# Routing a chunk inside attention: a mixed attention and expert kernel on one Trainium2 core

## The reference

```
x = x + 0.5 * expert(layernorm(x))      # experts, first time
x = x + attention0(layernorm(x))        # causal, 16 heads of 8, own wq, wk, wv, wo, bo
x = x + 0.5 * expert(layernorm(x))      # experts, second time
x = x + 0.5 * ternary(layernorm(x))
x = x + attention1(layernorm(x))        # causal, 16 heads, joint qkv with bias, no output projection
x = x + 0.5 * ternary(layernorm(x))

expert(h):  e = argmax(h @ Wr.T)        # 8 experts, one for each token
            y = gelu(h @ W1[e] + b1[e]) @ Wo + bo + h
            return layernorm(y) * gamma + beta
ternary(h): relu(h @ quantize(W1).T + b1) @ quantize(W2).T + b2
```

## Time and profile before

| | us |
|---|---|
| median of 3 runs | 1184.02 (1182.99 to 1186.48) |
| profiled execution, its time | 1181.55 |
| its span from first to last instruction | 1179.7 |
| TensorE matmuls busy | 1058.8 (90%) |
| VectorE busy | 973.2 (82%) |
| ScalarE busy | 662.1 (56%) |
| GpSimd busy | 100.6 (9%) |
| load of a sorted tile (64 KB), issue to landing | 1.8 |
| store of sorted rows (256 KB) | 2.3 |
| load of query rows (512 KB) | 3.7 |

### The profile page before, as it was taken

One profiled execution on the slowest core, in us unless ns is written; L12 is line 12 of the kernel. 1 busy time (PEld: TensorE's weight loads), 2 busy tenths in 40 slices (PEclk: granted clock), 3 DMA queues, 4 the chain that ended last, 5 costly groups with the idle time before them and its releaser, 6 DMA issues.

```text
span 1179.7 us, 34486 instructions
## 1 busy us (share of the span) xinstructions
PE 1058.8 (90%) x14718; PEld 484.9 (41%) x14718; DVE 973.2 (82%) x2307; ACT 662.1 (56%) x852; POOL 100.6 (9%) x124
## 2 busy tenths in 40 slices
PE   4989968999999999999788848699999999999988
PEld 2545533333333333334447726233333333333436
DVE  7786579999999999986535766899999999998843
ACT  3322214556777777787414213256677777787763
POOL 1530010000000000000043152000000000000000
PEclk9999989999999999999898979899999999999999
DMA  5061142000000000000011032210000000000001
GB/s 163 2 274 47 48 141 65 3 3 2 3 2 2 3 3 3 2 3 3 1 39 38 25 90 81 86 43 3 3 2 3 3 2 2 3 2 3 3 3 37
DMA packets 29493, 36.68 MB, mean 31 GB/s; under 512 B 3694, under 2 KB 26388, under 8 KB 29084
## 3 DMA queue, kind: packets, MB, share of 16 engines
q1 hardware_dynamic: 27228, 29.22, 7.4%
q0 software_dynamic: 2112, 5.25, 1.7%
HBM read 15.29 MB, written 18.87 MB: 29 GB/s over the span
## 4 chain that ended last, share of the span: by engine, by line
PE 50%; DVE 38%; issue 4%; ACT 3%; DMA 1%; SPq 1%; another core or an unknown queue 1%; POOL 0%; DVEq 0%; ACTq 0%; POOLq 0%
DVE part_max L2071 28%; PE psum L1930 12%; PE psum L1951 11%; PE psum L1901 6%; PE psum L520 5%; PE psum L1916 2%; PE psum L1583 2%; ACT hidden L2033 2%; PE psum L1978 1%; DVE xn L204 1%; PE psum L1182 1%; PE psum L544 1%; PE psum L1957 1%; PE psum L1573 1%; PE psum L299 1%
## 5 line engine op out<-in xcount | busy, mean ns | idle before, releaser
L2071 DVE TENSOR_REDUCE part_max<-psum 128x1 f32<-128x512 f32 (+3 forms) x1120 | 675.6, 669 | 37.5 <-PE psum L1957 21.8
L2033 ACT ACTIVATE hidden<-psum 128x1024 f32<-128x1024 f32 (+3 forms) x640 | 539.1, 895 | 221.4 <-PE psum L1901 220.6
L1951 PE MATMUL psum<-k_slots,q_slots 128*32 128x512 f16 (+3 forms) x5120 | 389.1, 353 | 27.8 <-DVE part_max L2071 15.1
L1930 PE MATMUL psum<-hidden,v_aug 128*9 128x512 f32 (+3 forms) x2560 | 291.3, 532 | 0.1
L1951 PEld LDWEIGHTS psum<-k_slots,q_slots 128*32 128x32 f16 x5120 | 123.0, 95 | 285.2 <-DVE part_max L2071 202.2
L1901 PE MATMUL psum<-q_slots,k_slots 32*128 32x512 f16 (+3 forms) x1472 | 140.5, 328 | 9.5 <-ACT hidden L2033 7.9
L520 PE MATMUL psum<-parts,w_parts 128*128 128x512 f16 x384 | 91.2, 389 | 3.8 <-DVE parts L945 3.8
L1957 PE MATMUL psum<-ident_bf,later_keys 128*32 128x128 bf16 (+2 forms) x1408 | 90.2, 247 | 0.0
L1901 PEld LDWEIGHTS psum<-q_slots,k_slots 32*128 32x128 f16 x1472 | 42.0, 91 | 98.7 <-ACT hidden L2033 46.3
L1916 PE MATMUL psum<-later_keys,ident_bf 128*32 128x128 bf16 x2048 | 75.1, 223 | 4.4 <-ACT hidden L2033 1.9
L1930 PEld LDWEIGHTS psum<-hidden,v_aug 128*9 128x9 f32 x2560 | 61.8, 91 | 34.5 <-ACT hidden L2033 1.9
(11 more groups left out here) (278 smaller groups left out, 846.8 us busy)
## 6 DMA issues: line engine op xcount, KB each, us to landing
expert_regions<-k_slots SPq DMA_DIRECT2D x2, 4096.0 KB, 17.8
q_slots<-q_rows SPq DMA_DIRECT2D x8, 512.0 KB, 3.7
k_slots<-k_rows POOLq DMA_DIRECT2D x28, 128.0 KB, 4.1
q_slots<-in_L_ffn_W_dram SPq DMA_DIRECT2D x2, 1024.0 KB, 6.4
q_rows<-parts SPq DMA_DIRECT2D x6, 256.0 KB, 2.6
k_rows<-parts SPq DMA_DIRECT2D x6, 256.0 KB, 2.7
q_slots<-expert_regions SPq DMA_DIRECT2D x20, 64.0 KB, 1.8
sorted_rows<-xn SPq DMA_DIRECT2D x5, 256.0 KB, 2.3
```

The source lines that it names most:

```text
L1930: last = pe.matmul(psum[VW * h:VW * h + DH + 1, O_BANK, off:CH], v_aug[:, j, G * g + h, :], probs[:, (2 * n + h // 2) % NP, h % 2, off:CH] ...
L1951: last = pe.matmul(psum[rows32(m), bank, a * w:(a + 1) * w], q_slots[:, g, qb * P + m * SLOT:qb * P + (m + 1) * SLOT], k_slots[:, G * g + ...
L2033: act.activation(probs[:, tile % NP, :, off:CH], psum[:, bank:bank + 2, off:CH], ACT.Exp, scale=scale).then_inc(exp_done, 1)
L2071: dve.tensor_reduce(part_max[:, step_no[s] % 2, h0:h0 + heads, i, kc], psum[:, bank, 0:heads * w].rearrange("p (a k) -> p a k", a=heads), ...
```

## The change

1. *Dense chunk inside attention 0.* A new class `DenseChunk` holds the dense chunk's buffers, semaphores and steps. Two ring items are added: "dense turn" in turn 158 (turn on PE, two copies on ScalarE behind that turn's exponentials, low part on DVE) and "dense logits" in turn 160 (four matmul blocks on PE, copy and choice on DVE). In turn 167 PE makes mask 0 before the last projection; DVE adds the bias before it waits for the projection, for all projections, and at the last one it also masks the input for expert 0 there.
2. *Sorting layer reordered.* PE starts with mask 1 and expert 0, without waiting for `released`; the wait, the choices' turn and the turns of the early chunks stand in the middle of expert 0, their logits behind it, ranks, late turn, late logits, ranks and tables in and behind experts 1 to 4. One mask bank (4) serves all masks instead of two.
3. *One turn later.* `features.turn(pe, 0)` comes behind the down projection of the last group of tiles.
4. *Ternary layer 1.* DVE's low part 1 comes before the whole norm of the next chunk, not between its statistics and its end.
5. *Last ternary layer.* Ring items "feature" 0 and 1 in turns 158 and 160 of attention 1: turn on PE, high part on ScalarE, low part on DVE. The up projection of chunk 0 is issued in turn 164, behind the last values, before the last output is turned. The layer then starts with up 1 and waits for `released` only before its third turn.

```diff
+            def mask_of(self, pe, e):
+                pe.wait_ge(self.chosen, 1)
+                if e >= 1:
+                    pe.wait_ge(self.mask_ready, e)
...
-                pe.wait_ge(*released)
                 early = batches[0]
-                turn(dense, PREP_BANK)
-                turn(early[0], BATCH_BANK)
-                turn(early[1], SPARE_BANK)
-                logits([dense], PREP_BANK)
-                logits(early, BATCH_BANK)
-                pe.wait_ge(chosen, 1)
-                for e in range(AHEAD_E):
-                    mask_of(e)
-                choices()
...
+                def beside(e):
                     if e == 0:
+                        dense_chunk.mask_of(pe, 2)
+                        pe.wait_ge(*released)
+                        choices()
+                        turn(early[0], BATCH_BANK)
+                        turn(early[1], SPARE_BANK)
+                    if e == 1:
+                        ranks(0, BATCH_BANK)
+                    if e == 2:
+                        logits([late], PREP_BANK)
+                    if e == 3:
+                        ranks(1, PREP_BANK)
+                    if e == 4:
+                        table(2)
+
+                def following(e):
+                    if e == 0:
+                        logits(early, BATCH_BANK)
+                    if e == 1:
                         pe.wait_ge(choices_out, 1)
                         turn(late, PREP_BANK)
+                    if e + 3 < E:
+                        dense_chunk.mask_of(pe, e + 3)
+                    if e == 3:
+                        table(1)
+                    if e == 4:
+                        table(3)
+
+                dense_chunk.mask_of(pe, 1)
+                for e in range(E):
+                    masked_expert(e, lambda: beside(e))
+                    following(e)
                 table(4)
                 biases()
...
+                    down(n)
                     if n == TGROUPS - 1:
                         features.turn(pe, 0)
-                    down(n)
...
                     following.low_parts(dve, 0)
-                    norms.begin(dve, own, s1, order[2])
                     features.low_part(dve, 1)
-                    norms.end(dve, own, s1, order[2])
+                    norms.make(dve, own, s1, order[2])
...
+            if dense:
+                ahead_items = [("dense turn", 0), ("dense logits", 0)]
+            else:
+                ahead_items = [("feature", 0), ("feature", 1)]
...
+                RING_ITEMS[-1] += {LAST_QUAD - 5: ahead_items[:1], LAST_QUAD - 3: ahead_items[1:]}.get(len(RING_ITEMS) - 1, [])
...
+                        if dense and item == final:
+                            dense.mask_of(pe, 0)
                         ring_item(item)
...
+                    if features and turn == LAST_QUAD + 1:
+                        pe.wait_ge(ring_read, ring_no["feature", 0] + 1)
+                        features.up(pe, 0)
...
+                        if kind == "project":
+                            rows = x_res[:, what * BPC:(what + 1) * BPC, :]
+                            own(dve.tensor_tensor(rows, rows, bcast_blocks(bo_bc, BPC), ALU.add))
+                            if item == final:
+                                dense.masked(dve, 0)
                         dve.wait_ge(ring_full, n + 1)
```

More of the change, by code:

```diff
@@ L1148, in sorted_turn @@
                     else:
[L1149 removed]
+                        pe.wait_ge(mask_ready, E)
                     for i in range(BPC):
@@ new lines, in low_part_of, with up @@
+            def low_part_of(self, dve, n, bank):
+                dve.wait_ge(self.hi_ready, n + 1)
+                return dve.scalar_tensor_tensor(out=self.x_parts[:, n % 2, 1, :], in0=psum[:, bank, :], scalar=X_SCALE,
+                                                in1=self.x_parts[:, n % 2, 0, :], op0=ALU.mult, op1=ALU.subtract)
+            def low_part(self, dve, n):
+                self.low_part_of(dve, n, 4 + n % 2).then_inc(self.lo_ready, 1)
+            def up(self, pe, n, relu_done=None):
+                if n >= self.begun:
+                    pe.wait_ge(self.lo_ready, n + 1 - self.begun)
+                for t in range(HT):
+                    if n >= 1:
+                        pe.wait_ge(relu_done, HT * (n - 1) + t + 1)
+                    for xp in range(2):
+                        last = pe.matmul(psum[:, t, :], tw1_t[:, t, :], self.x_parts[:, n % 2, xp, :],
+                                         start=(xp == 0), stop=(xp == 1))
+                    last.then_inc(self.up_done, 1)
@@ L1567, in up @@
                 def up(n):
[L1568 to L1575 removed]
+                    features.up(pe, n, relu_done)
                 def down(n):
@@ L1605, in _ @@
                 else:
-                    pe.wait_ge(*released)
-                    features.turn(pe, 0)
-                    for n in range(NCH):
+                    pe.wait_ge(*features.last_split)
+                    for n in range(1, NCH):
                         up(n)
+                        if n == 1:
+                            pe.wait_ge(*released)
                         if n + 1 < NCH:
                             features.turn(pe, n + 1)
-                        if n >= 1:
-                            down(n - 1)
+                        down(n - 1)
                     down(NCH - 1)
@@ L1687, in _ @@
                 else:
-                    late = list(norms.order[given:])
-                    for n in range(NCH - 1):
-                        features.low_part(dve, n)
-                        if late:
-                            norms.make(dve, own, s1, late.pop(0))
+                    norms.begin(dve, own, s1, order[NCH - 1])
+                    features.low_part(dve, 2)
+                    norms.end(dve, own, s1, order[NCH - 1])
                     dve.wait_ge(norms.ready, NB)
@@ L1963, in ring_item @@
                         last = pe.transpose(psum[0:G * BPC, bank, 0:P], neg_max[:, k % 2, :], ident[:, :])
+                    elif kind == "dense turn":
+                        last = dense.turn(pe, bank)
+                    elif kind == "dense logits":
+                        last = dense.logits(pe, bank)
+                    elif kind == "feature":
+                        last = features.turn_into(pe, what, bank)
                     elif kind == "turned":
@@ L2041, in _ @@
                         act.copy(out_t[:, k % 2, :], psum[:, O_BANK, :]).then_inc(out_copied, 1)
+                    for kind, what in items:
+                        n = ring_no[kind, what]
+                        if kind == "dense turn":
+                            act.wait_ge(ring_full, n + 1)
+                            dense.copies(act, RING_BANKS + n % RING)
+                        elif kind == "feature":
+                            act.wait_ge(ring_full, n + 1)
+                            features.high_part_of(act, what, RING_BANKS + n % RING)
             @blk.vector
@@ L2066, in _ @@
                         bank = RING_BANKS + n % RING
-                        dve.wait_ge(ring_full, n + 1)
-                        if kind == "scores":
+                        if kind == "project":
[3 more added lines that the diff above has]
+                                dense.masked(dve, 0)
+                        dve.wait_ge(ring_full, n + 1)
+                        if kind == "dense turn":
+                            dense.low_part(dve).then_inc(ring_read, 1)
+                            dve.wait_ge(ring_read, n + 1)
+                        elif kind == "dense logits":
+                            dve.tensor_copy(dense.logit[:, 0:BPC, :],
+                                            psum[:, bank, 0:BPC * E].rearrange("p (b e) -> p b e", e=E)).then_inc(ring_read, 1)
+                            dve.wait_ge(ring_read, n + 1)
+                            dense.choose(dve, own, dense.place, BPC, NPART)
+                        elif kind == "feature":
+                            features.low_part_of(dve, what, bank).then_inc(ring_read, 1)
+                        elif kind == "scores":
                             s, i, kc, h0, heads = what
@@ L2076, in _ @@
                         elif kind == "project":
-                            rows = x_res[:, what * BPC:(what + 1) * BPC, :]
-                            own(dve.tensor_tensor(rows, rows, bcast_blocks(bo_bc, BPC), ALU.add))
                             own.wait()
```

255 lines of the change are left out of this document (131 added, 124 removed).

## The result

| | before | after |
|---|---|---|
| median of 4 runs, us | 1183.66 (1182.99 to 1186.48) | 1161.27 (1159.16 to 1164.12) |
| profiled execution, its time | 1181.55 | 1162.20 |
| its span | 1179.7 | 1160.4 |
| TensorE / VectorE busy | 1058.8 / 973.2 | 1054.0 / 972.7 |
| mean granted clock | 0.971 | 0.975 |

The medians differ by 22.4 us. The profiled executions differ by 19.3, against 19.0 forecast. TensorE and VectorE are busy for nearly as long as before; what went is mostly waiting.

What follows compares the result with a forecast made beforehand. The prediction took waits at five places, behind attention 0 through to the end, as what the change could shorten. Gains 0 + 9.0 + 4.1 + 0 + 5.9 = 19.0 us gave 1162.6 profiled, 1165.0 for the median, range 1159 to 1173.

Steps and rivals of the forecast that it cites:

- what attention 0 pays: Dense chunk's added work inside attention 0: 0.7 lost against clock won back, taken as 0, ends 1.2 lost and 0.7 won.
- part 1: Dense chunk moved inside attention 0, sorting layer reordered: sorted-row loads start earlier, 9.0 us gained, ends 5.3 and 10.
- part 2: Turn placed behind the last sorted group's down projection, which then needn't wait: 4.1 us gained, ends 3.0 and 4.3.
- part 3: Low part before the norm in ternary layer 1: 0 gained, ends 1.5 lost and 2.5 won.
- part 4: Last ternary layer's first two splits moved into attention 1: 6.8 less 0.9 paid there, 5.9 us gained, ends 5.3 and 7.
- Boundary: Behind attention 0: first masked expert starts at 578.5 instead of 588.56, 10 us earlier; first scatter from 588.5 instead of 594.55.
- the scatters become what is late: Sorting: table complete at 601.3 without late signals, scatters land 605.6, so loads start at 605.7 instead of 615.20: 9.5 us.
- rival A: Signals to DVE and ScalarE late twice or more on the table's chain: 9.0 becomes 5.4, time 1168.6; chance 0.27.
- The further 0.3: Sorting: TensorE's pause at 617 to 621 shrinks and with it time at the lower clock, 0.3 us gained.
- Rival B: Maskings and choices beside scatters lock GpSimd out of the shared port, lengthening scatters by 1.5 to 2 us: 1167; chance 0.10.
- Rival D: Some ten TensorE signals beside scatters each late by 3.0: 30 lost against 19 won, 1195, slower; chance 0.03.
- the 0.9 that attention 1 was to pay: Two turns and two high parts added in attention 1, 1.2 in all, less 0 to 1.4 for clock: 0.9 lost.

Runs made afterwards that it cites:

- the second chip: Chip of four follow-up kernels: scatters held back, tiny probe operations, idle matmuls in the changed kernel or with the last-layer edit undone; the kernel before took 1177.58 there.
- without part 3: Changed kernel with DVE's low part 1 in ternary layer 1 again between the statistics and the end of the norm: 1163.35, ratio 0.986.
- the held version: Changed kernel with GpSimd waiting for the finished table before the first scatter: 1168.24, and 1170.67 when run again on a third chip.
- without parts 2, 3 and 4: Three kernels, each the changed kernel with one edit undone (later turn, ternary layer 1's low part, last ternary layer): 1168.29, 1163.35, 1173.76.
- the kernel without part 4: Changed kernel without the two feature items in attention 1 and the up projection ahead: 1173.76, ratio 0.993.

## Why the prediction was right, and where it was not

Predicted 1165.0 (1159 to 1173), measured 1161.27. By the profiled executions the sum was 1162.6 and the time is 1162.2. The sum is right because its errors cancel:

| term | forecast | before to after | with the part taken away |
|---|---|---|---|
| what attention 0 pays | 0 | 0.4 gained | 0.6 gained |
| part 1 at the boundary and in sorting | 9.0 | 6.6 | 7.2 |
| part 2 | 4.1 | 3.9 | 4.2 |
| part 3 | 0 | 1.0 | 1.1 |
| part 4 with attention 1 | 5.9 | 7.3 | 9.1 |

(Part 1 from the last maximum to the first down projection of sorted rows, 72.4 before and 65.8 after; part 2 from there to the `x_plus` addition behind group 4, 44.1 and 40.1; part 3 from there to attention 1's first maximum, 74.2 and 73.2; part 4 from there to the end, 433.1 and 425.8.) They sum to 19.3 with 0.04 from the start. That the sum comes so close is luck in part: part 1 was forecast 2.4 too high, parts 3 and 4 together 2.4 too low.

**Attention 0** pays nothing, as taken. The drop of the clock in 560 to 570 is gone: the window stands at 1.00 in after, and a drop comes behind it instead.

**Boundary.** Expert 0 came 10.3 earlier, forecast 10. The first scatter came 6.8 earlier, forecast 6; the twelfth at 602.19, forecast 603.1; SyncE's reads took 2.42, forecast 2.4. These steps held.

**The term that was mis-sized** is part 1's 9.0, and in it "the scatters become what is late", with one late signal of 3.0 to 3.2 assumed on the table's chain. There was one, but 5.9 long, so the table was late (605.5) and not the scatters; rival A's mechanism with one event in place of two, though it priced two at 5.4 where 6.6 came. The price of one signal was also too low by the prediction's own figures: 3.0 to 3.2 against a slack of 2.0 (603.7 to 605.7) cost 1.0 to 1.2, not 0.8. Without a late signal the step holds: on the second chip the loads start 50.7 and 50.1 behind the last maximum, where the forecast's 605.7 is 49.7. With it they stand at 52.4 and 54.0. The further 0.3 for the clock in 617 to 621 didn't come: the clock averages 0.76 in the 14 us from 606 in after, as in the 14 us from 613 before.

**How long the late signals last.** All traces with late signals at the table have one thing in common. In the kernel before (timeline, 608 to 613), the last scatter is issued from 609.19 to 610.16, and TensorE had finished the table's third step at 608.95:

```profile
612.12 0.17 DVE L1405 TENSOR_TENSOR tile_f<-psum,tile_rank 1x20 f32<-1x20 f32 x1 [2.79 <-remote]
```

VectorE takes it up 2.0 us after the issue of the last scatter ended. In after this is 1.7 us, without part 3 it is 2.1, and in all nine traces with late signals there it is 1.7 to 2.1, though TensorE had finished at very different times, from 4.2 us before the end of that issue to 0.3 behind it. So a fixed length of 3.0 to 3.2 was the wrong model: the table came when the scatters were over, and the loads start 5.6 to 6.1 behind the start of the last scatter in all nine (5.9 before, 5.7 in after), against 2.3 to 3.1 in the traces of the second chip. What part 1 brought to the loads, 7.3 us, is by this reading the 7.0 by which the scatters moved. It is read from the traces; no run was made to test it.

**Rival B, the port rule.** The Trainium skill (SBUF — State Buffer, section "SBUF: two separate sides") gives the shared port, for the whole instruction, to whichever of the two engines starts first. The prediction charged every masking in full, also those that begin while a scatter runs, which the page doesn't ask for. Three maskings fell beside scatters, not four, which the prediction's reading of the rule would price at 2.1. The twelve scatters take 1.004 us on average in after and 0.988 in the held version, with one masking beside them: 0.2 in all. Only a masking that began just ahead of a scatter cost something (592.77 and 592.97: 1.33 instead of 0.96). Those begun while a scatter ran (589.25 and 596.18) cost nothing, as the page has it for GpSimd. But they weren't blocked by the scatter either: the one at 589.25 started as soon as its mask was copied and took its usual 0.69. The row was the better guide.

**Rival D** asked for late signals beside scatters from ten of TensorE's signals. The mechanism exists, but with at most five of them in a trace, several released together, and none beside the first five scatters. In the traces without parts 2, 3 and 4 it also held TensorE up, by 1.7 and 2.8 us, without moving the loads by more than 0.5.

**Part 2** is right in each step: the down projection without a wait, the turn covered, 4.2 forecast for the down's end.

**Part 3** failed in one step: "since the turn's place is set by the norm, which doesn't move". The norm's statistics had waited 1.55 in the earlier trace rows, and the low part fills that wait. The turn came 1.7 earlier against the `x_plus` addition (36.8 behind it before, 35.1 after), and the lower clock on the down projection took 0.7 back (5.36 against 4.61 without part 3). The result lies inside the ends given.

**Part 4.** 23.0 forecast from the last values to the end, 22.6 measured. What was wrong is the 0.9 that attention 1 was to pay: it was 0.45 by the kernel without part 4, and the fall of the clock in the earlier trace rows stayed away, which gave 1.3 that don't belong to the part. The larger worth with the part taken away is the clock again, 2.8 of it.

**The median.** The forecast put it 2.5 above the profiled execution, as before. It is 0.9 below it. The same kernel's medians differ by 0.7 between two chips, before's by 6, so this last addition had no ground.

## What to carry to other kernels

Read which wait ends last after the change as carefully as the one you remove. Here the gain at the loads was 7 and not the 9.5 of the forecast without late signals, because a late signal, which the trace of before already showed twice, stayed on the path. Its length changed, but its end hardly moved against the end of the last scatter (2.0 before, 1.7 after). So compare the end of an unexplained wait with what else ends near it before carrying its length over. Place a step that waits for another engine behind the work that doesn't need it: one turn moved by a line gave 4 us, some by the wait and the rest by a clock that no longer fell behind it. And cut both traces at the same instructions: spans differ by 4 us for code that nobody touched.

## What the hardware did that was not expected

**TensorE's signals come late beside GpSimd's indirect DMAs, on some chips.** In the second half of twelve scatters, signals to ScalarE and VectorE came 2 to 6 us late and several at once, the last of them 1.7 to 2.1 us after the issue of the last scatter had ended; with the scatters moved away they came within 0.1. Two of the three chips of the experiments had them in every trace whose scatters lay beside the experts (four and three traces), the third in none of three. The kernel before was 3 to 4 us faster on the chip without them (1177.58 against 1181.35 and 1180.74), which fits, though it wasn't traced there. With more work on TensorE they also appeared beside the indirect DMAs that fetch rows back. A profile of an engine shows when it computes, not when its signal is seen; the Trainium skill (Perfetto Trace Analysis, section "Per-instruction lifecycle: what the profiler-reported window actually captures") says that propagation of a semaphore lies outside the window. These rows fit that, since no engine's row covers the 5.9 us. What holds the signal back isn't settled: the scatters were necessary in the one comparison made on one chip, dense work of TensorE beside them is suggested by one kernel, and the chip or something that goes with it decides.

**The clock fell behind short pauses.** In the last layer without part 4, waits of 0.7 to 1.4 us between dense pieces came with 10 us at half clock (0.53 on average over 11 us). With six idle matmuls in each of two waits it stayed at 1.00 in that stretch, worth 2.8 us. But idle matmuls didn't pay everywhere: with 66 of them in the changed kernel it was 3.7 us slower than without, on the same chip.
